# Top network of the first 128 batch columns moved into the middle of a three-layer interaction kernel, with one buffer of turned rows and newly set order tables

## The reference, cut to what matters

```python
def _L0_rec_ref(embeddings, W0, W1, W2):          # B, M, D = 512, 32, 16
    x0 = embeddings
    xk = x0
    outs = []
    for W in (W0, W1, W2):                        # each (32, 32 or 64, 64)
        xk = jax.nn.relu(jnp.einsum('bmd,bhd,mhk->bkd', x0, xk, W))
        outs.append(jnp.sum(xk, axis=2))
    return jnp.concatenate(outs, axis=1)
e = jnp.stack([tbl_0[ids[:, 0]], ..., tbl_31[ids[:, 31]]], axis=1)
z = _L0_rec_ref(e, L0_rec_W0, L0_rec_W1, L0_rec_W2)
h = jnp.concatenate([z.reshape(z.shape[0], -1), dense_ctx], axis=1)   # 3 * 64 + 16 = 208
h = jnp.maximum(h @ W_top1 + b_top1, 0.0)         # 208 -> 512
h = jnp.maximum(h @ W_top2 + b_top2, 0.0)         # 512 -> 256
y = h @ W_top3                                    # 256 -> 1
```

## Time and profile before

| what | value |
|---|---|
| three runs | 338.79, 339.94 and 414.93 us; median 339.94 |
| span of the profiled execution | 356.2 us (no other time is given for that execution) |
| PE busy | 314.8 us, 88%, 1602 matmul records |
| DVE busy | 282.1 us, 79%, 172 instructions |
| POOL busy | 246.0 us, 69%, 195 instructions |
| ACT busy | 53.3 us, 15% |
| DMA | 68.09 MB, 191 GB/s over the span |
| mean granted clock of PE | 0.990 |

### The profile page before, as it was taken

The page is one execution under the profiler, slowest core; times in us unless marked ns, Lnnn a source line. Parts: engine busy times, 40 slices in busy tenths (PEclk is TensorE's granted clock), DMA queues, the critical chain, the costliest instruction groups (busy, mean ns, idle before and its releaser), DMA issues.

```text
span 356.2 us, 4290 instructions
## 1 busy us (share of the span) xinstructions
PE 314.8 (88%) x1602; PEld 114.9 (32%) x1602; DVE 282.1 (79%) x172; ACT 53.3 (15%) x77; POOL 246.0 (69%) x195
## 2 busy tenths in 40 slices
PE   0378588988699788898999999998999999999997
PEld 0344224432222223332333333332333333333334
DVE  0039477869499878999999999999998879999220
ACT  1000011012020221110112120121022111220011
POOL 5646566766367668869997987896998569729300
PEclk9999989999899999999999999999999999999999
DMA  6272853834875982979499989683699897050000
GB/s 183 65 231 72 230 154 73 230 71 110 295 240 174 326 292 65 326 217 280 167 317 289 296 284 297 201 268 67 215 346 337 290 291 194 17 133 2 0 0 0
DMA packets 34302, 68.09 MB, mean 191 GB/s; under 512 B 5866, under 2 KB 15082, under 8 KB 34282
## 3 DMA queue, kind: packets, MB, share of 16 engines
q1 hardware_dynamic: 23562, 56.80, 49.0%
q10 hardware_dynamic: 6624, 9.96, 9.4%
q0 software_dynamic: 4096, 1.06, 3.5%
HBM read 55.55 MB, written 2.03 MB: 162 GB/s over the span
## 4 chain that ended last, share of the span: by engine, by line
PE 59%; POOL 16%; issue 11%; DVE 9%; another core or an unknown queue 2%; DMA 1%; DVEq 1%; ACT 0%; POOLq 0%; SPq 0%
PE acc L1060 37%; PE acc L1055 12%; POOL gathered L719 10%; DVE vz L805 8%; POOL pz L746 6%; PE factor L984 2%; PE factor L1093 2%; PE factor L1021 1%; PE factor L1088 1%; PE acc L1050 1%; PE factor L998 1%; PE acc L1082 1%; PE factor L1100 1%; DVEq L800 1%
## 5 line engine op out<-in xcount | busy, mean ns | idle before, releaser
L805 DVE TENSOR_TENSOR vz<-fields_sb,factor 128x1024 f32<-128x1024 f32 (+3 forms) x113 | 230.5, 2090 | 20.7 <-PE factor L984 7.6
L1060 PE MATMUL acc<-vz,w_sb 128*64 128x512 f32 (+1 forms) x800 | 172.6, 569 | 10.9 <-DVE vz L805 3.6
L719 POOL DMA_INDIRECT gathered<-in_table,index x128 | 121.6, 950 | 65.0 <-issue 31.5
L746 POOL TENSOR_TENSOR pz<-fields_sb,hidden 128x1024 f32<-128x1024 f32 (+1 forms) x52 | 117.9, 2292 | 19.4 <-DMA hidden<-relu_out 9.6
L1060 PEld LDWEIGHTS acc<-vz,w_sb 128*64 128x64 f32 x800 | 57.8, 139 | 113.7 <-issue 98.6
L1055 PE MATMUL acc<-vz,w_sb 128*64 128x512 f32 x216 | 60.9, 621 | 3.7 <-DVE vz L805 2.9
L1060 PE MATMUL acc<-pz,w_sb 128*64 128x512 f32 x192 | 48.1, 594 | 0.3 <-POOL pz L746 0.3
L934 ACT ACTIVATE relu_out<-acc 128x512 f32<-128x512 f32 (+1 forms) x30 | 15.3, 512 | 126.3 <-PE acc L1060 47.3
L890 ACT ACTIVATE factor<-hidden 128x1024 f32<-128x1024 f32 (+1 forms) x23 | 20.1, 878 | 65.8 <-DMA hidden<-relu_out 34.3
L805 DVE TENSOR_TENSOR vz<-rotated,factor 128x2048 f32<-128x2048 f32 x12 | 26.9, 2279 | 1.8 <-issue 1.8
L1055 PEld LDWEIGHTS acc<-vz,w_sb 128*64 128x64 f32 x216 | 16.4, 139 | 36.4 <-issue 24.6
(11 more groups left out here) (44 smaller groups left out, 83.2 us busy)
## 6 DMA issues: line engine op xcount, KB each, us to landing
fields_sb<-fields SPq DMA_DIRECT2D x48, 512.0 KB
rotated<-fields SPq DMA_DIRECT2D x24, 512.0 KB
fields_sb<-fields SPq DMA_DIRECT2D x32, 256.0 KB
hidden<-relu_out ACTq DMA_DIRECT2D x30, 256.0 KB, 5.6
own<-fields SPq DMA_DIRECT2D x6, 512.0 KB
gathered<-in_table,index POOLq DMA_INDIRECT x128
hidden<-relu_out ACTq DMA_DIRECT2D x16, 128.0 KB
fields<-gathered SPq DMA_DIRECT2D x6, 256.0 KB, 5.2
```

What stands on the lines that cost most here:

```text
L719: nc.gpsimd.indirect_dma_start(gathered[:, pair % GRING, j, :], None, table, bass.IndirectOffsetOnAxis(ap=index[:, i:i + 1], axis=0)).then ...
L746: nc.gpsimd.tensor_tensor(pz[:, at % PRING, 0:cols], fields[s][:, t, col:col + cols], hidden_of(step, g), ALU.mult).then_inc(pz_ready, 1)
L805: nc.vector.tensor_tensor(vz[:, at:at + nt, 0:cols].rearrange("p t (a n) -> p t a n", n=half), src[:, t:t + nt, col:col + cols].rearrange( ...
L1060: last = nc.tensor.matmul(acc_of(step, ab), w_sb[layer][:, kt, :], z[:, ab * half:(ab + 1) * half], start=start and j == 0, stop=stop and ...
```

## The change

The first two pairs of blocks (blocks 0 to 3, 128 batch rows) get their top network in the middle: eight loads of top weights ("weights") and six small loads of sums ("early") join SP's order, and 18 matmuls of 128 columns join TensorE's around the start of step (2,4), in a slot of the factor ring of their own. ScalarE applies their relus. The top network at the end runs on the other 384 columns. The top weights get places of their own; `rotated` becomes one buffer for both streams, and its loads wait for VectorE's layer 0 of the block before. The order tables are set anew: among them seven paired steps become one, and five `SPREAD` and seven `HALF` steps become five and five others.

```diff
-TOP_LOADS = 9 * 16
+TOP_LOADS = 11 * 16
+EARLY_PAIRS = 2
+EARLY = 2 * EARLY_PAIRS * CHUNK
+LATE_HALF = (PAIRS - EARLY_PAIRS) * CHUNK
+LATE = 2 * LATE_HALF
...
-BEGUN = [(0, 0), (1, 0), (0, 1), (2, 0), (0, 2), (1, 1), (0, 3), (1, 2), (2, 1), (2, 2), (1, 3), (0, 4), (0, 5),
-    (2, 3), (1, 4), (1, 5), (2, 4), (0, 6), (2, 5), (0, 7), (1, 6), (1, 7), (0, 8), (2, 6), (2, 7), (0, 9), (1,
-    8), (1, 9), (2, 8), (2, 9)]
+BEGUN = [(0, 0), (1, 0), (0, 1), (2, 0), (0, 2), (1, 1), (0, 3), (1, 2), (2, 1), (2, 2), (0, 4), (1, 3), (0,
+    5), (2, 3), (1, 4), (1, 5), (2, 4), (0, 6), (2, 5), (0, 7), (1, 6), (1, 7), (2, 6), (0, 8), (2, 7), (0,
+    9), (1, 8), (1, 9), (2, 8), (2, 9)]
+TOP_STEP = (2, 4)
+TOP_AT = (-3, -3, -2, -2, -1, -1, 2)
+TOP_ITEMS = [("top1", m) for m in range(F_TOP1 // P)] + [("top2", m) for m in range(F_TOP2 // P)] + [("y", 0)]
+TOP_FACTOR = (("top", 0), 0)
-SPREAD = [(1, 0), (2, 3), (1, 4), (1, 5), (1, 9)]
-HALF = [(2, 0), (1, 2), (2, 2), (1, 3), (2, 4), (1, 7), (2, 7)]
+SPREAD = [(1, 0), (2, 0), (2, 1), (1, 3), (2, 3)]
+HALF = [(2, 2), (1, 6), (1, 7), (2, 6), (2, 7)]
-    (1, 5): 5, (2, 4): 3, (2, 5): 4, (1, 6): 4, (1, 7): 3, (2, 6): 4, (2, 7): 5, (1, 8): 6, (1, 9): 4, (2, 8): 3,
+    2, (1, 5): 2, (2, 4): 4, (2, 5): 4, (1, 6): 4, (1, 7): 3, (2, 6): 4, (2, 7): 6, (1, 8): 4, (1, 9): 6, (2,
-    (0, 1, 0, 2), (1, 7): (3, 4, 0), (0, 8): (8,)}
+    0, 2, 0), (0, 8): (1,), (2, 7): (1, 0, 0, 0, 0, 0)}
-PACED = {12: 1, 13: 2, 14: 4, 17: 5, 18: 6, 19: 7, 20: 8, 22: 9, 24: 11, 25: 14, 26: 15, 28: 16, 29: 17, 30: 18,
+PACED = {10: 2, 12: 2, 13: 2, 14: 2, 17: 4, 18: 6, 19: 9, 21: 9, 23: 9, 25: 11, 27: 12, 28: 14, 30: 16, 31:
-BEHIND_SPREAD = {10: 1, 11: 3, 15: 4, 24: 5, 26: 6, 36: 7, 43: 8, 45: 9, 55: 10, 61: 11, 80: 12, 85: 13, 93: 14}
+BEHIND_SPREAD = {14: 1, 15: 4, 26: 4, 31: 4, 55: 8, 71: 8, 72: 11, 76: 11, 77: 11, 101: 11, 105: 11, 114: 11,
-PAIRED = [(2, 0), (1, 1), (1, 2), (2, 1), (2, 2), (1, 3), (2, 3)]
+PAIRED = [(1, 3)]
...
-        rotated = [sb(f"rotated{s}", [P, L0TILES, PAIR]) for s in range(STREAMS)]
+        rotated = sb("rotated", [P, L0TILES, PAIR])
...
+                if b - 1 not in DIRECT + BURST:
+                    sp.wait_ge(vz_ready, vectors_to((0, b - 1)))
                 for t in range(L0TILES):
-                    if second_half(b):
-                        sp.wait_ge(rotated_in[s][t], rotated_count(b - 1))
...
+            def early_sums():
+                last = max(b for b, block in enumerate(BLOCKS) if block[0] < EARLY_PAIRS)
+                for layer in range(3):
+                    sp.wait_ge(sums_done, max(ORDER.index((layer, b)) for b in range(last + 1)) + 1)
+                    to, first = (early2, 0) if layer == 2 else (early01, layer * HID)
+                    for ab in range(2):
+                        sp.dma_start(to[first:first + HID, ab * (EARLY // 2):(ab + 1) * (EARLY // 2)],
...
+            def early_top(what, m):
+                if what == "top1":
+                    if m == 0:
+                        pe.wait_ge(top_in, TOP_LOADS)
+                        pe.wait_ge(early_in, 96)
+                        pe.wait_ge(vz_ready, factor_free(TOP_FACTOR))
+                    to = early_bank(0)[:, m * EARLY:(m + 1) * EARLY]
+                    nc.tensor.matmul(to, wt1_sb[:, m * P:(m + 1) * P], early01[:, :], start=True, stop=False)
+                    last = nc.tensor.matmul(to, wt1e_sb[:, m * P:(m + 1) * P], early2[:, :], start=False, stop=True)
```

More of the change, by code:

```diff
@@ L229, in tensor_program @@
                 program.insert(at - 1 if step == BEGUN[0] and g == 1 else at, (step, "wave", g))
+    for n, (what, m) in enumerate(TOP_ITEMS):
+        made = VECTOR[top_after(n) - 1]
+        at = program.index((made[0], "v", made[1])) + 1
+        while program[at][1] in ("spread", "top1", "top2"):
+            at += 1
+        program.insert(at, (TOP_FACTOR[0], what, m))
     for step in PAIRED:
@@ L530, in rotated_count @@
         def rotated_count(b):
-            return 16 * sum(1 for a in range(b + 1) if a not in DIRECT + BURST and stream(a) == stream(b))
+            return 16 * sum(1 for a in range(b + 1) if a not in DIRECT + BURST)
         def operands_in(b):
```

160 lines of the change are left out of this document (111 added, 49 removed), and 11 rows, old and new, of the table PACED.

## The result

The changed kernel takes 357.84 us (median of 4 runs, 357.16 to 358.04) against 339.49 us before: 1.0537 times as long, 95% interval 1.0512 to 1.0563. The forecast was 336.0 us with a range up to 346; both the sign and the range were wrong. The comparisons here are with that second trace.

A forecast was written before the change was run, and what follows sets the result against it. Bounds: chain and loads in narrow blocks, full TensorE from about 180 us, TensorE alone in the tail. Tail -3.8, early network +1.1, spreads +1.1, GpSimd's order -1.3, narrow blocks -1.0 make -3.9: 336.0 us, range 328 to 346.

The forecast's parts named there:

- The narrow blocks: Narrow blocks: removed VectorE waits against later gathers and a later spread of (2,3); -1.0 us, between -8 and +4.
- 8.0 us of gains: Three VectorE waits in the narrow blocks, at 97.43, 126.94 and 141.79 us, have causes removed; together 8.0 us.
- The new delays: Narrow blocks: gather 15 later, and `own` of block 1 with it, 3.3 us; (2,3)'s spread, +1.3 us.
- One buffer at nothing: Loads of `rotated` for blocks 5, 7 and 9 wait for VectorE; cost nothing, since other steps stand between.
- The early network: Early top matmuls in (1,5) and the start of (2,4): 3.9 us of TensorE, mostly hidden; +1.1 us.
- the other end: Early network if TensorE is full in that stretch: +3.9 us instead of +1.1.
- the room of 5.7 us: TensorE around (1,5) and (2,4): 2.3 us idle plus 3.4 us of spreads that leave, for 3.9 us of work.
- The tail: Final top network on TensorE, 384 columns instead of 512: -3.8 us, between -4.0 and -3.0.
- The four spreads later on: Three wide spreads become four, of (1,6), (1,7), (2,6), (2,7), where TensorE is full: +1.1 us.
- GpSimd's order at (0,8): TensorE's 1.32 us gap at (0,8)'s opposite part goes, with one gather ahead instead of eight: -1.3 us, between -1.3 and +2.
- The slower one: Rival: the single buffer holds SP up, so VectorE waits for `fields` in (1,4), (1,6), (1,8); 348 us, chance 0.18.
- three handovers of 4 us: In the slower rival: VectorE waits some 4 us for `fields` ahead of each of (1,4), (1,6) and (1,8).

The follow-up runs named there:

- second trace: The kernel before, run unchanged again for another trace, whose span is 338.7 us; measured 340.55 us.
- e18: Kernel before with the change's narrow steps (six of seven paired steps plain, spreads in (2,0), (2,1), (1,3), one GpSimd tile moved): 339.40 us, ratio 1.0005.
- e2: Kernel before with one buffer of turned rows, old tables and the top network at the end: 353.40 us, ratio 1.0405.
- e12: Changed kernel with its last four gathers moved ahead of products of (1,7): 359.29 us, ratio 1.0593 to the kernel before.
- e3: Kernel before with all new tables, without weights and early sums, two buffers, top network at the end: 360.37 us, ratio 1.0571.
- e6: Kernel before with all new tables and one buffer of turned rows, top network at the end: 356.95 us, ratio 1.0408.
- e15: Kernel before with factors of (1,4), (1,5) and (2,4) by relay in place of spreads on TensorE: 346.52 us, ratio 1.0223.
- e17: Kernel before with (2,6) ahead of (0,8) and the eight last gathers ahead of the first product of (2,6): 344.87 us, ratio 1.0150.
- e14: Kernel before with the last gather moved from ahead of (0,8)'s opposite product to ahead of the first product of (2,7): 349.04 us, ratio 1.0303.
- e4: Changed kernel with the top weights' loads moved on SP's queue ahead of scratch of block 3: 356.55 us, ratio 1.0493 to the kernel before.
- e20: Changed kernel with (0,8) ahead of (2,6) again, its gathers too, and top weights issued by ScalarE ahead of (1,0)'s relu: 357.12 us, no ratio.
- e9: Kernel before with the new gather tables alone: 362.02 us, ratio 1.0685.
- e13: Changed kernel with weights early, operands 3 and gathers as before, except the last eight, ahead of products of (1,7) and (2,6): 369.57 us, ratio 1.0904.

## Why the prediction was wrong

The sum was -3.9 us, and the spans differ by +17.5. By stretch: -0.9 ahead of (1,0), +7.2 from there to (1,4), +9.1 to (2,4), +2.5 to (1,8), -0.4 to the end.

**The narrow blocks: the step that failed.** I took -1.0 us, between -8 and +4; measured is +7.2 from (1,0) to (1,4). Both halves failed. The 8.0 us of gains were read from the first trace: in the second the wait of 4.86 us, which I put in (2,2) and which stands at the last products of (2,1), is 0.55 us, the one at (0,5) 1.75, and none stands ahead of (1,4), 2.3 us in all. And paired steps made plain, the cause that I named for two of them, change nothing at the end: in e18 (2,2) starts 2.6 us earlier than before, and (1,4) at the same time (125.5 and 125.4 us). The new delays I priced at gather 15 and stopped there. That price was right (29.11 instead of 25.88 us, 3.2 us later), and it cost next to nothing: VectorE's wait in (0,1) is 1.86 instead of 1.17 us. But the tables move all gathers: the last one of block 5 is 6.9 us later, and the rows of every block pass through SP's queue, where `fields` of other blocks stand behind them. VectorE pays 5.6 us at (0,5) for `rotated` of block 5, 3.43 us at (0,3), and 5.99 us at (1,4), past the end of this stretch.

**One buffer at nothing: the second that failed.** Alone it costs 13.9 us (e2), with (0,4) directly ahead of (0,5). In the changed order "work stands between" held as far as it went: (0,7) and (0,9) do not wait for their rows. But SP stands still for the buffer from 173.8 to 189.0 us ahead of `rotated` of block 7, `fields` of block 6 begin at 193.5 instead of 170.5 us, and VectorE waits 1.84 us for them in (1,6); with the gathers early (e12) it is the buffer that holds block 9. On the Trainium skill's rule that I weighed ("Trainium Kernel Development and Optimization", section Best Practices: double-buffer, so that loads overlap compute): e2 agrees, with 13.9 us; with the new tables a second buffer gives nothing that can be measured (e3, 355.98 to 360.64 us, against e6, 351.53 to 362.96), most likely since other delays of the same loads cover it. The rule tells the sign, not whether the price is already paid.

**The early network: moved, not hidden.** I took +1.1 and named 3.9 as the other end. In the changed kernel:

```profile
163.06 0.49 PE L1175 MATMUL factor<-early,wt_sb 128*128 128x128 f32 x2
...
164.15 1.08 PE L1142 MATMUL acc<-pz,w_sb 128*64 128x512 f32 x4
...
170.69 2.05 PE L1182 MATMUL factor<-early_top,wt_sb 128*128 128x128 f32 x16
```

Two first-layer groups take 163.06 to 164.15, two more as long, the second layer 2.0 us, the output 0.5: 4.7 us, in a stretch in which TensorE has no gap from 144.49 us on. Of the room of 5.7 us that I counted, the 3.4 of the spreads did leave; the 2.3 of idle time a late TensorE no longer has. More of the 9.1 us lost in this stretch is VectorE's: the wait of 5.99 us on `fields`, which the sum had at nothing and only a rival named, and two tiles more ahead of (2,4), 2.2 us, where I had counted one over the three steps. **The tail** gives back 3.3 us, not 3.8:

```profile
341.27 0.86 PE factor L1239 x8
...
353.87 0.26 DVE vz L939
```

12.6 us against 15.9. On TensorE the move itself is a small loss, 4.7 against 3.3 us. What it costs in the whole is not shown: e6 is the changed kernel without it, and its runs, 351.53 to 362.96 us, lie on both sides of 357.84. No wait for the early sums shows ahead of them; that part was right.

**Spreads and relays.** I counted three spreads less in (1,4) to (2,4) as room, and nothing for the relays in their place. Alone they cost 7.2 us (e15); in the changed order (1,4) does not wait for its relay. The four spreads later on were not run alone; from (2,4) to (1,8) the changed kernel loses 2.5 us in all.

**GpSimd's order at (0,8).** The gap that I counted as -1.3 us is not in the second trace of before: TensorE is busy 20.00 of 20 us from 240 to 260 there, as it is in the changed kernel. So there was nothing to gain, and that the sign I named came true says nothing. The swap that goes with it costs 5.5 us alone (e17), and I looked only at the product behind the gathers, not at the scratch behind them: one gather is worth 10 us (e14).

**The rivals.** The slower one had the mechanism, SP held up, with the right signs to look for: waits on `fields` in (1,4) and, small, in (1,6), and (1,4) 7.2 us later against (1,0), where I had set 4. It had a chance of 0.18 and 348 us. It was too small because it counted three handovers of 4 us (5.99 us came at (1,4), 1.84 at (1,6), and no wait on a load at (1,8)) and not the gathers. The weights alone are not the cause either: earlier on SP's queue (e4) or on ScalarE's (e20) they give nothing that was measured. The Trainium skill says that another issuer saves issue time only, since the DMAs of all engines run on the same 16 engines ("DMA: Bandwidth & Descriptors", section "Issuing engines are not separate DMA queues"); no run here shows it, since e20 also issues the weights some 85 us sooner.

## What to carry to other kernels

Read the queue that issues the loads as an engine of its own: list its issues with their starts, and for every instruction that a change moves ask which load it releases and which loads stand behind that one. Do the same for an engine that issues and computes: a gather ahead of GpSimd's product (e9, e13) or a relay ahead of ScalarE's put (e15) makes the work behind it late. Price a table of order by its latest load and not by the engine waits that it removes, and take waits to be removed from a trace whose span agrees with the median of the runs. Expect one part alone to cost as much as all of them together, and repairing one to give nothing, where several delays cover each other.
